# A recommendation model on one core: four rounds of Gram matmuls ahead of four rounds of top layers

## What is computed

```python
x = mlp(dense_x, bot)                        # 13 -> 512 -> 256 -> 64, ReLU
pooled = vmap(lambda tab, ix: take(tab, ix, axis=0).sum(axis=1))(tables, indices)
Tcat = concatenate([x[:, None, :], transpose(pooled, (1, 0, 2))], axis=1)   # 27 vectors of 64
Z = einsum('bim,bjm->bij', Tcat, Tcat)       # Gram matrix of each sample
li, lj = tril_indices(27, k=-1)
R = concatenate([x, Z[:, li, lj]], axis=1)   # 64 + 351 = 415 features
y = mlp(R, top)                              # 415 -> 512 -> 256 -> 1, sigmoid at the end
```

## Time and profile before

| | before |
|---|---|
| median of 3 runs | 2874.72 us (2874.49 to 2882.71) |
| profiled execution, its own time | 2880.54 us |
| span of its trace | 2878.7 us |
| TensorE's granted clock, mean over the span | 0.960 |
| PE busy | 2756.6 us, 96% |
| ACT, DVE, POOL busy | 2113.8, 1995.2, 1805.9 us |

### The profile page before, as it was taken

One profiled execution on the slowest core, in us unless ns is written; L12 is line 12 of the kernel. 1 busy time (PEld: TensorE's weight loads), 2 busy tenths in 40 slices (PEclk: granted clock), 3 DMA queues, 4 the chain that ended last, 5 costly groups with the idle time before them and its releaser, 6 DMA issues.

```text
span 2878.7 us, 65596 instructions
## 1 busy us (share of the span) xinstructions
PE 2756.6 (96%) x24204; PEld 1309.0 (45%) x24204; DVE 1995.2 (69%) x3358; ACT 2113.8 (73%) x2496; POOL 1805.9 (63%) x1640
## 2 busy tenths in 40 slices
PE   5999999999999999999999999999999999999798
PEld 2344444444444444444444444444444444448574
DVE  4477787877878778787777877778777778734121
ACT  2678878788787787877878878788787887853232
POOL 3277777777777777777777777777777777200000
PEclk8999999999999999999999999999999999996668
DMA  2112122121221212212122121121221212118611
GB/s 69 62 32 76 31 76 74 32 76 30 76 74 32 76 29 77 75 30 76 42 64 76 31 78 55 49 77 29 78 73 33 76 29 76 31 29 129 119 31 31
DMA packets 173102, 167.99 MB, mean 58 GB/s; under 512 B 116104, under 2 KB 134328, under 8 KB 167476
## 3 DMA queue, kind: packets, MB, share of 16 engines
q1 hardware_dynamic: 121380, 110.94, 13.8%
q0 software_dynamic: 51200, 52.53, 8.0%
q10 hardware_dynamic: 272, 0.52, 0.1%
HBM read 143.83 MB, written 20.05 MB: 57 GB/s over the span
## 4 chain that ended last, share of the span: by engine, by line
PE 82%; ACT 11%; issue 3%; SPq 1%; DMA 1%; ACTq 1%; DVE 1%; DVEq 0%; POOL 0%; POOLq 0%
PE ps L693 58%; PE ps L674 14%; ACT counts L841 6%; PE ps L637 5%; PE ps L766 4%; ACT parts L803 4%; ACT parts L810 1%; SPq L509 0%; ACT h_bot L854 0%; DMA pooled<-pooled_sb 0%; ACTq L838 0%; SPq L532 0%; DMA look_in<-in_r_indices 0%; DMA products<-zt 0%; SPq L516 0%
## 5 line engine op out<-in xcount | busy, mean ns | idle before, releaser
L611 POOL DMA_INDIRECT rows<-in_L_rec_tables,look x1600 | 1788.8, 1118 | 622.9 <-issue 453.1
L841 ACT CAST counts<-ps 128x792 int32<-128x792 f32 (+1 forms) x1848 | 1712.3, 984 | 476.2 <-PE ps L674 463.5
L693 PE MATMUL ps<-counts,parts 128*128 128x512 fp8e3 x8232 | 2024.3, 389 | 0.0
L693 PEld LDWEIGHTS ps<-counts,parts 128*128 128x128 f16 x8232 | 719.2, 96 | 914.8 <-issue 11.5
L1058 DVE TENSOR_TENSOR onehot_p<-iota_by_unit,place 128x1024 bf16<-128x1024 bf16 x924 | 638.5, 691 | 395.4 <-PE ps L674 367.3
L674 PEld LDWEIGHTS ps<-onehot_c,onehot_p 60*128 60x128 bf16 x14448 | 370.5, 95 | 482.3 <-ACT counts L841 276.3
L674 PE MATMUL ps<-onehot_c,onehot_p 60*128 60x99 bf16 x14448 | 522.7, 208 | 56.1 <-ACT counts L841 39.2
L1063 DVE TENSOR_TENSOR onehot_c<-column_c,weighted_s 128x792 bf16<-128x792 bf16 x924 | 521.4, 564 | 0.0
L1019 DVE SCALAR_TENSOR_TENSOR raw<-raw,coef_next,parts 128x896 f32<-128x896 f32 x147 | 169.1, 1150 | 59.7 <-ACT parts L803 59.7
L1092 DVE TENSOR_REDUCE rows<-rows 128x64 f32<-128x384 f32 (+1 forms) x240 | 189.9, 791 | 13.9 <-DVE pooled_sb L1069 13.9
L394 DVE COPY zt<-ps 32x208 f32<-32x208 f32 x128 | 64.8, 507 | 151.0 <-PE ps L766 149.1
(11 more groups left out here) (82 smaller groups left out, 529.3 us busy)
## 6 DMA issues: line engine op xcount, KB each, us to landing
raw<-in_L_rec_tables SPq DMA_DIRECT2D x21, 1792.0 KB
raw<-in_L_rec_tables SPq DMA_DIRECT2D x21, 1344.0 KB
rows<-in_L_rec_tables,look POOLq DMA_INDIRECT x1600
pooled<-pooled_sb SPq DMA_DIRECT2D x84, 128.0 KB
slots<-pooled SPq DMA_DIRECT2D x30, 352.0 KB, 7.9
products<-zt SPq DMA_DIRECT2D x16, 351.0 KB
idx_raw<-in_r_indices SPq DMA_DIRECT2D x42, 79.7 KB
gathered<-bags_t SPq DMA_DIRECT2D x42, 64.0 KB
```

Source lines behind the costliest of these rows:

```text
L611: nc.gpsimd.indirect_dma_start(rows[:, s, l, :], None, rows_flat, bass.IndirectOffsetOnAxis(ap=look[:, c, s * PL + l:s * PL + l + 1].bitca ...
L693: mm = nc.tensor.matmul(acc[k % 2][:, 0:NB], parts[:, j, :], count_bytes[k % 2][:, j % COLS, 0:NB, j // COLS], start=(j == 0), stop=(j == ...
L841: nc.scalar.copy(counts[k % 2][:, :, u * UG * GS:(u * UG + g) * GS].rearrange("p c (g h s) -> p h g c s", h=HALVES, s=HS), unit_ps[unit_bu ...
```

## The change

It rewrites the order of the tail on PE and ACT: first the four rounds of Grams, then the four rounds of top layers. The wait for the top layers inside `make_grams` goes, and the wait for the copied Grams moves out of `top_mlp` to one place between the two parts. Nothing is added or removed among matmuls, copies, activations and transfers, and the streams of DVE, GpSimd and SP stay as they are.

```diff
@@ make_grams @@
                     if b >= 4:
                         pe.wait_ge(diag_act, b - 2)
                         pe.wait_ge(diag_dve, b - 2)
-                    if r >= 2 and b == r * GRAMS_PER_TILE + 2:
-                        pe.wait_ge(top_act, TOP_STEPS * (r - 1))
                     for x in range(GRAMS):
...
             def top_mlp(r):
                 pe.wait_ge(dense_in, 16 * TILES)
                 pe.wait_ge(pairs_in[r], 16 * NPIECE)
-                done = GRAMS_PER_TILE * min(r + 2, TILES)
-                pe.wait_ge(diag_act, done)
-                pe.wait_ge(diag_dve, done)
                 mlp(top_tiles, top_banks, top_mm, top_act, TOP_STEPS * r, TOP_STEPS * (r + 1))
 
-            make_grams(0)
-            for r in range(1, TILES):
+            for r in range(TILES):
                 make_grams(r)
-                top_mlp(r - 1)
-            top_mlp(TILES - 1)
+            pe.wait_ge(diag_act, NGRAM)
+            pe.wait_ge(diag_dve, NGRAM)
+            for r in range(TILES):
+                top_mlp(r)
...
@@ scalar engine @@
-            diagonals(0)
-            for r in range(1, TILES):
+            for r in range(TILES):
                 diagonals(r)
-                top_activations(r - 1)
-            top_activations(TILES - 1)
+            for r in range(TILES):
+                top_activations(r)
```

## The result

| | before | changed |
|---|---|---|
| median | 2875.66 us (4 runs, 2874.49 to 2882.71) | 2850.69 us (4 runs, 2849.20 to 2854.84) |
| ratio, with its 95% interval | | 0.991 [0.9891, 0.993] |
| profiled execution, its own time | 2880.54 us | 2854.84 us |
| span of its trace | 2878.7 us | 2853.0 us |
| the tail: first Gram to the end of PE's last matmul | 2875.91 - 2608.43 = 267.48 us | 2850.24 - 2602.98 = 247.26 us |

The kernel is about 25 us faster by its medians, 0.9%. The two traces lie 25.7 us apart: 20.2 us in the tail, which is where the change is, and 5.5 us in the first part, in which not one instruction was touched: the first Gram starts at 2602.98 in place of 2608.43. The two have to be explained apart.

The account below looks back on a forecast made before the run. PE was taken to pace the tail, idle 14.29 us for `feats`. Savings of 14.29, 2.37, 0.34 and 3.9, less 0.1 for `slots`, made 20.8 us off the median 2874.72: 2853.9 us, range 2849 to 2862.5.

Parts of the forecast that it names:

- The wait of 14.29 us: PE's idle time for `feats` ahead of the top layers of round 0; predicted to vanish, saving 14.29 us.
- Two stretches at half clock: First top layers behind Grams begin at clock 0.50; two of three such stretches predicted to go, saving 3.9 us.
- One wait for copies: PE's wait between Grams and top layers for the last copies; one of two predicted to go, saving 2.37 us.
- The wait for `slots` 3: PE ahead of round 3's Grams, loads queued behind round 0's round trip; taken as 0.1 us, between nothing and 2.7.
- The small gain that I thought possible: Round 3's `slots` loads issued faster beside Grams, last landing 1.1 us earlier, PE's wait for them down to nothing.
- The sum: All terms of the tail on PE together: 20.8 us less, PE ending at 2855.1 in place of 2875.91.
- top round 0: First round of top layers, behind the Grams, beginning at clock 0.50; taken as 27.8 us from start to next start.
- The case in which the first part falls otherwise: Unchanged long first part scatters; median lies with the slowest run, 2861.9 us; chance 0.08.
- The rival with full clock: Four rounds of Grams raise the clock, so round 0's top layers take 25.9 us, total 2852.0; chance 0.03.
- The rival that ends slower: Clock stays at 0.50 in the top layers after 139 us of Grams; 2949 us if it never rose; chance 0.02.

Follow-up runs that it names:

- grams2_early: Against the kernel before, only the Grams of round 2 moved ahead of the top layers of round 0; ratio 0.9944, tail 249.83 us.
- grams3_early: Against the kernel before, only the Grams of round 3 moved ahead of the top layers of round 1; ratio 0.9979, tail 263.34 us.

## Why the prediction was right

**The wait of 14.29 us** was PE's order, not a limit of the transfers: `feats` of round 0 came when they came, and PE had work that it was not allowed to start. Moving one round of Grams ahead removes it (grams2_early), and it shows up nowhere else. The step stands.

**Two stretches at half clock**, 3.9 us by the sum, were 4.56 us between the two traces: two first layers that fell by about 1.9 each, and 0.7 in the first one, which varies from 16.8 to 17.9 us behind Grams. The step stands: grams3_early shows one such layer fall by itself, and the changed kernel's row with 151 GB/s shows that transfers beside it don't slow it.

**One wait for copies**, 2.37 us, was 2.52.

**The wait for `slots` 3** was put at 0.1 us, with 2.7 as the upper bound; it was 1.50, 0.58 and 0.51 us in three traces. This is the term that was mis-sized. Its landing was at the lower end of the predicted range (2.55 us behind the beginning of the last issue). But the round trip of round 0 ahead of it in the queue, which I had taken over from the earlier trace rows unchanged, took 1.7 us longer: counted from the first Gram, the load began at 2682.73 - 2602.98 = 79.75 us, and at 2686.49 - 2608.43 = 78.06 before. Of this, 0.9 us lie ahead of the loads of `feats`, in the stores and the wait for them: the loads begin at 69.13 us in place of 68.24, and between 68.2 and 68.8 in the other traces with this order of the queue, among them the kernel before run again. The other 0.8 us are the issuing of `feats`, 10.57 us in place of 9.78. It took 10.5 to 10.95 us in the four traces where Grams run beside it and 9.77 to 9.92 in the three where PE stands idle through most of it. But Grams alone can't be the reason: `feats` of round 1 were issued in 9.72 us beside Grams before and in 9.81 beside Grams now. The cause stays open. The small gain that I thought possible, faster loads beside Grams, didn't come: 16.29 + 7.23 us as before.

**The sum** was -20.8 us for the tail and came out at -20.2. In part that is luck: the wait for `slots` took 1.4 us more than predicted, and 0.8 us came back from terms that were a little too large, 0.5 of it in top round 0 (27.29 us from start to start, where 27.8 was taken). The predicted time of 2853.9 us lies 3.2 above the measured median. If the tail repeats there as in the traces, the first part was shorter in those runs. The case in which the first part falls otherwise did occur, but with the other sign: I had priced only its bad side.

**The rival with full clock** is out: the clock was 0.50 through 138 us of Grams. The Trainium skill, TensorE: Matmul & The Clock Gate, Part 1, has sustained matmul work release the throttle; here 138.61 us of nearly unbroken Grams didn't, while top layers did within 4 us. **The rival that ends slower**, a clock that stays low, is out as well: behind the longest stretch of Grams the first layer was no slower than behind the shorter ones (17.18 and 16.25 us behind 138.28 us of Grams, 17.33 and 17.25 behind 34.82).

## What to carry to other kernels

An engine's stream is a queue: where it waits for a round trip, look for independent work behind the wait, and check what bounds that work (buffers, banks, the transfer queue) before it is moved. Here one round of work was enough to cover the trip. The second round paid only through one wait for copies and one slow first layer less (tails of 249.83 and 247.26 us), and brought the next limit, a load queued behind the same round trip. Where kernels differ by less than a per cent, split the span at the first touched instruction: what moved ahead of it isn't explained by the waits that the edit took away, and the unchanged kernel has to be run again to see how much it scatters.

## What the runs showed of the hardware

The loop of the first part has turns of two lengths. The same two turns of the changed kernel, one long and one short, with their granted clock, then 6 us around the beginning of each (columns as above), and PE's rows there:

```profile
597.56:717.15 119.59, 117.06 (x1089) 52.82 (x1087) 91.99 (x154) 96.09 (x111) 89.60 (x81) 0.99 0.22 58
717.15:835.33 118.18, 115.50 (x1088) 52.33 (x1086) 91.90 (x153) 95.70 (x111) 89.92 (x81) 1.00 0.22 58
```

```profile
596.00:598.00 2.00, 1.28 (x20) 0.79 (x21) 2.00 (x4) 1.35 (x2) 0.11 (x1) 0.96 0.26 58
598.00:600.00 2.00, 2.00 (x6) 0.52 (x4) 2.00 (x4) 1.87 (x3) 0.00 (x0) 0.50 0.20 21
600.00:602.00 2.00, 2.00 (x21) 1.05 (x21) 2.00 (x4) 1.22 (x2) 0.78 (x1) 0.68 0.00 0
...
714.00:716.00 2.00, 0.68 (x4) 0.10 (x1) 1.31 (x4) 1.98 (x3) 0.94 (x1) 1.00 0.39 82
716.00:718.00 2.00, 1.84 (x22) 1.01 (x23) 2.00 (x4) 1.49 (x3) 0.00 (x0) 1.00 0.14 25
718.00:720.00 2.00, 2.00 (x24) 0.92 (x23) 2.00 (x4) 2.00 (x3) 0.00 (x0) 1.00 0.23 21
```

```profile
596.72 0.56 PE L674 MATMUL ps<-onehot_c,onehot_p 60*128 60x99 bf16 x16 [1.96 <-DVE onehot_c L1058]
597.21 3.05 PE L693 MATMUL ps<-counts,parts 128*128 128x512 fp8e3 x8
600.20 0.85 PE L674 MATMUL ps<-onehot_c,onehot_p 60*128 60x99 bf16 x16
...
716.16 0.57 PE L674 MATMUL ps<-onehot_c,onehot_p 60*128 60x99 bf16 x16 [1.48 <-ACT counts L837]
716.66 1.98 PE L693 MATMUL ps<-counts,parts 128*128 128x512 fp8e3 x8
718.57 0.56 PE L674 MATMUL ps<-onehot_c,onehot_p 60*128 60x99 bf16 x16
```

At the seam between turns PE pauses in both, 1.96 us in one and 1.48 in the other. Behind the first pause the clock falls to 0.50 for some 3 us: eight matmuls of L693 take 3.05 us in place of 1.98, the next sixteen of L674 0.85 in place of 0.56, and the turn takes 1.4 us more. In the other turn the clock stays at 1.00. Between 0 and 8 of 18 turns of a trace are of the long kind. In these nine traces the start of the first Gram mostly follows their number; executions of one kernel differ by up to 10.5 us, which is more than several of the terms above.

That Grams don't gain from a full clock was not expected either. The Grams of round 3 before begin behind a top round, at a clock of 1.00, and the clock falls 3 to 4 us into them though PE doesn't pause:

```profile
2785.00:2788.00 3.00, 3.00 (x23) 2.96 (x24) 0.00 (x0) 0.68 (x1) 0.00 (x0) 1.00 0.00 0
2789.00:2822.00 33.00, 30.86 (x230) 30.60 (x228) 16.21 (x32) 15.86 (x32) 0.00 (x0) 0.50 0.00 1
```

They take 34.82 us. The Grams of round 3 in the changed kernel stand alone behind a wait, at 0.50 from the beginning, and take 34.82 us as well. In all these rows the weight loads (PEld) are busy nearly all of the time that the Grams take, 69.05 of 70 us in the changed kernel; that they set the pace fits this and was not tried.
